# A damped-attention tower on one core: the two terms of the weighted sum in column halves, the sine product on GpSimd, all rows normalised on VectorE

## The reference, cut to what matters

```python
def qrt_damping(x):
    return jnp.sin(C1 * x) * jnp.exp(-(x * x) / PHI) + jnp.cos(C2 * x)
def ttt_filter(scores):
    int_scores = (jnp.abs(scores) * PHI_INT).astype(jnp.int32)
    mod9 = int_scores % 9
    chaos = (mod9 == 0) | (mod9 == 3) | (mod9 == 6)
    return scores * jnp.where(chaos, PHI_INV, 1.0)
...
scores = ttt_filter(jnp.einsum('bhqd,bhkd->bhqk', q, k) / 8)
attn = jax.nn.softmax(scores, axis=-1)
attn = attn * qrt_damping(attn)
ctx = jnp.einsum('bhqk,bhkd->bhqd', attn, v)
```

## Time and profile before

| | |
|---|---|
| median of 3 runs | 6793.55 us (6787.77 to 19916.96) |
| the profiled execution | 6774.6 us |
| its span in the profile | 6772.9 us |
| granted TensorE clock, mean | 0.892 of full speed |
| DMA, whole span | 48.46 MB, 7 GB/s |

### The profile page before, as it was taken

One profiled execution on the slowest core, in us unless ns is written; L12 is line 12 of the kernel. 1 busy time (PEld: TensorE's weight loads), 2 busy tenths in 40 slices (PEclk: granted clock), 3 DMA queues, 4 the chain that ended last, 5 costly groups with the idle time before them and its releaser, 6 DMA issues. The chain is left out here.

```text
span 6772.9 us, 115321 instructions
## 1 busy us (share of the span) xinstructions
PE 5442.1 (80%) x32426; PEld 3955.2 (58%) x32489; DVE 5082.3 (75%) x10177; ACT 4262.2 (63%) x7370; POOL 2754.5 (41%) x2639
## 2 busy tenths in 40 slices
PE   2788877787777877877888777778787799997999
PEld 1455555555555555555655555555555577775777
DVE  1888888888888888888888888888888555555443
ACT  1677777777777777777777777777777322222222
POOL 4445554444555544444555444445554200100111
PEclk9888898989889888888888889888988799898999
DMA  1000000000000000000000000000000000000000
GB/s 17 12 8 7 7 7 7 7 7 10 7 7 7 7 7 7 7 9 9 7 7 7 7 7 7 9 9 7 7 7 4 8 1 2 1 1 13 4 6 6
DMA packets 34500, 48.46 MB, mean 7 GB/s; under 512 B 24473, under 2 KB 24537, under 8 KB 34010
## 3 DMA queue, kind: packets, MB, share of 16 engines
q1 hardware_dynamic: 31962, 43.49, 2.5%
q0 software_dynamic: 2048, 0.14, 0.1%
HBM read 39.40 MB, written 4.19 MB: 6 GB/s over the span
## 5 line engine op out<-in xcount | busy, mean ns | idle before, releaser
L571 PE MATMUL banks<-ident,att 128*128 128x128 f32 x8192 | 1458.9, 311 | 873.6 <-DVE ag L508 496.8
L571 PEld LDWEIGHTS banks<-ident,att 128*128 128x128 f32 x8192 | 1024.2, 159 | 1568.6 <-DVE ag L508 1044.0
L377 POOL TENSOR_TENSOR sinb<-sinb,work 128x512 f32<-128x512 f32 x1024 | 1289.3, 1272 | 900.3 <-DVE sinb L482 898.3
L599 PE MATMUL banks<-kT,qT 128*128 128x512 f32 x2048 | 1262.5, 702 | 113.9 <-ACT att L423 104.0
L387 POOL TENSOR_SCALAR wgt<-wgt 128x512 f32<-128x512 f32 x1024 | 700.2, 684 | 1586.7 <-DVE wgt L502 1581.4
L635 PEld LDWEIGHTS outp<-vo,sinb 128*128 128x128 f32 x8192 | 1164.7, 216 | 214.9 <-issue 185.3
L635 PE MATMUL outp<-vo,sinb 128*128 128x64 f32 x8192 | 1162.6, 295 | 1.9 <-ACT att L423 1.9
L476 DVE TENSOR_TENSOR work<-banks,work 128x512 f32<-128x512 f32 x1024 | 699.8, 689 | 254.0 <-ACT work L435 183.6
L451 ACT ACTIVATE work<-banks 128x512 f32<-128x512 f32 x1024 | 609.9, 596 | 420.4 <-PE banks L571 411.6
L458 ACT ACTIVATE mag<-banks 128x512 f32<-128x512 f32 x1024 | 606.4, 594 | 356.2 <-PE banks L599 350.0
L435 ACT ACTIVATE work<-banks,halfpi 128x512 f32<-128x512 f32 x1024 | 695.4, 685 | 208.9 <-PE banks L571 139.6
(11 more groups left out here) (194 smaller groups left out, 6740.6 us busy)
## 6 DMA issues: line engine op xcount, KB each, us to landing
xq<-xT_dram SPq DMA_DIRECT2D x64, 256.0 KB
xv<-xT_dram SPq DMA_DIRECT2D x64, 256.0 KB, 3.7
xT_dram<-xT SPq DMA_DIRECT2D x8, 256.0 KB, 2.9
out<-hres SPq DMA_DIRECT2D x8, 256.0 KB, 2.6
base<-in_L_tok_turns,idx POOLq DMA_INDIRECT x64
wqk<-in_L_attn_Wq SPq DMA_DIRECT2D x64, 16.0 KB
wqk<-in_L_attn_Wk SPq DMA_DIRECT2D x64, 16.0 KB
wqk<-in_L_attn_bq SPq DMA_DIRECT2D x64, 0.2 KB
```

Source lines behind the costliest of these rows:

```text
L377: nc.gpsimd.tensor_tensor(sinb[:, k % RING], sinb[:, k % RING], work[:, k % RING], ALU.add).then_inc(summed, 1)
L571: mm = nc.tensor.matmul(bank[:, i * P:(i + 1) * P], att[:, p, 4 * half + i, kt * P:(kt + 1) * P], ident[:], is_transpose=True, start=(i == ...
L599: nc.tensor.matmul(score_bank(n), qT[:, p, (n // 2) * P:(n // 2 + 1) * P], kT[:, p, (n % 2) * 512:(n % 2 + 1) * 512], start=True, stop=Tru ...
```

## The change

1. The weighted sum. The value block `vo[:, kt]` becomes the stationary operand (64 columns), and `work` (cosine term) and `sinb` (sine term) are each streamed whole, 512 columns; the first goes to rows 0 to 63 of `outp`, the second to rows 64 to 127. GpSimd's sum of the terms is gone. A tile k now has key block k % 8 and query half k // 8, so `outp` holds one query half at a time and is taken out twice a head (OUT): copied to `acc` for an even head, added to it for an odd head. Every second head `acc` is multiplied with `pair` (two identities on top of each other), which adds the two terms and transposes back (FOLD, 8 matmuls), and VectorE adds the result to `hres` (ADD).
2. The sine goes to `sinb` in SBUF; the bank is free once the sine has read it. GpSimd multiplies `sinb` by `ag`, VectorE's L482 is gone.
3. VectorE normalises all eight rows; the rounding of turns starts one step earlier (TURNS). GpSimd's L382 is gone.
4. The schedule: projections at steps 24 and 26 instead of 18 and 20, values at 29 instead of 25, AV at steps 34 to 41 and then 44, 46 to 58.
5. `kT` has one buffer for both parities, the other head's rows meeting zeros of `qT`.

The diff, cut to its core:

```diff
+        kT = sb("kT", [P, S])
+        acc = sb("acc", [P, 2, 512])
+        pair = sb("pair", [P, D])
...
-        PROJ, VAL = 18, 25 + STEPS
+        PROJ, VAL = 24, 29 + STEPS
...
-        AV = [SINE + 6 + 8 * k // 5 for k in range(NTILE)]
-        OUT = AV[-1] + 1
+        AV = [SINE + 6 + k if k < TB else SINE + 16 + 2 * (k - TB) for k in range(NTILE)]
+        OUT = (AV[TB - 1] + 1, AV[-1] + 1)
+        FOLD, ADD = OUT[1] + 1, OUT[1] + 2
...
-        TURNS = EXP + 3
-        DVE_ROWS = (TB // 2 - 1, TB - 1)
+        TURNS = EXP + 2
...
+        def folds(g, p):
+
+            if isinstance(g, int):
+                return g // 2
+            return (g - p) // 2
...
-                        k = a - SINE - 5
+                        k = a - SINE - 4
                         if 0 <= k < NTILE:
-
-                            wait(pool, tmul, NTILE * g + k + 1)
-                            nc.gpsimd.tensor_tensor(sinb[:, k % RING], sinb[:, k % RING], work[:, k % RING],
-                                                    ALU.add).then_inc(summed, 1)
-                        j = a - EXP - 1
-                        if 0 <= j < TB and j not in DVE_ROWS:
-                            held(pool, recip, TB * g + j + 1)
-                            nc.gpsimd.tensor_scalar(att[:, p, j], att[:, p, j], rs[:, j:j + 1], TURN,
-                                                    ALU.mult, ALU.mult).then_inc(weights, 1)
+                            wait(pool, sined, NTILE * g + k + 1)
+                            wait(pool, agd, NTILE * (g + 1))
+                            nc.gpsimd.tensor_tensor(sinb[:, k % RING], sinb[:, k % RING], ag[:, k],
+                                                    ALU.mult).then_inc(tmul, 1)
...
                 if c == 0:
-                    wait(act, qk, NTILE * (g - 1))
+                    wait(act, qk, NTILE * g)
                 cols = slice(c * 512, (c + 1) * 512)
-                nc.scalar.activation(qT[0:D, p, cols], outp[0:D], ACT.Copy, scale=QSCALE).then_inc(qk_sb, 1)
-                nc.scalar.activation(kT[0:D, p, cols], outp[D:P], ACT.Copy).then_inc(qk_sb, 1)
+                rows = slice(p * D, (p + 1) * D)
+                nc.scalar.activation(qT[rows, p, cols], outp[0:D], ACT.Copy, scale=QSCALE).then_inc(qk_sb, 1)
+                nc.scalar.activation(kT[rows, cols], outp[D:P], ACT.Copy).then_inc(qk_sb, 1)
...
                             wait(act, nned, NTILE * g + k + 1)
-                            nc.scalar.activation(sine_bank(k), sine_bank(k), ACT.Sin,
+                            wait(act, av, NTILE * g + k - RING + 1)
+                            nc.scalar.activation(sinb[:, k % RING], sine_bank(k), ACT.Sin,
                                                  scale=2.0 * math.pi * (1.0 - 2.0 ** -22)).then_inc(sined, 1)
...
-                        k = a - SINE - 4
-                        if 0 <= k < NTILE:
-                            wait(dve, sined, NTILE * g + k + 1)
-                            wait(dve, av, NTILE * g + k - RING + 1)
-                            nc.vector.tensor_tensor(sinb[:, k % RING], sine_bank(k), ag[:, k],
-                                                    ALU.mult).then_inc(tmul, 1)
-                        if a == OUT:
-                            wait(dve, av, NTILE * (g + 1))
+                        if a in OUT:
+                            half = OUT.index(a)
+                            wait(dve, av, NTILE * g + TB * (half + 1))
+                            if p == 0:
+                                nc.vector.tensor_copy(acc[:, half], outp[:]).then_inc(evac, 1)
+                            else:
+                                nc.vector.tensor_tensor(acc[:, half], outp[:], acc[:, half], ALU.add).then_inc(evac, 1)
+                        if a == ADD and p == 1:
+                            wait(dve, folded, folds(g, p) + 1)
...
                         j = a - EXP - 1
-                        if j in DVE_ROWS:
+                        if 0 <= j < TB:
...
-                            wait(pe, turned, TB * (g + 1))
-                            kt, half = k // 2, k % 2
+                            wait(pe, turned, TB * g + 4 * (k // TB) + 4)
+                            kt, half = k % TB, k // TB
...
                             else:
-                                wait(pe, tmul, NTILE * g + k - 3)
-                            fill(g, p, sine_bank(k), k // 2, k % 2)
+                                wait(pe, sined, NTILE * g + k - 3)
+                            fill(g, p, sine_bank(k), k % TB, k // TB)
                         if a in AV:
                             k = AV.index(a)
-
-                            wait(pe, summed, NTILE * g + k + 1)
+                            kt, half = k % TB, k // TB
+
+                            wait(pe, acd, NTILE * g + k + 1)
+                            wait(pe, tmul, NTILE * g + k + 1)
                             if k == 0:
                                 wait(pe, v_sb, g + 1)
-                            kt, half = k // 2, k % 2
-                            for i in range(4):
-                                o = (4 * half + i) * D
-                                mm = nc.tensor.matmul(outp[:, o:o + D], sinb[:, k % RING, i * P:(i + 1) * P],
-                                                      vo[:, kt, :], start=(k == 0 and i == 0),
-                                                      stop=(k >= NTILE - 2), skip_group_check=True)
+                            if k == TB:
+                                wait(pe, evac, 2 * g + 1)
+                            for term, rows in ((work, slice(0, D)), (sinb, slice(D, P))):
+                                mm = nc.tensor.matmul(outp[rows], vo[:, kt, :], term[:, k % RING],
+                                                      start=(kt == 0), stop=(kt == TB - 1), skip_group_check=True)
                             mm.then_inc(av, 1)
+                        if a == FOLD and p == 1:
+                            wait(pe, evac, 2 * g + 2)
+                            for j in range(TB):
+                                mm = nc.tensor.matmul(outp[:, j * D:(j + 1) * D],
+                                                      acc[:, j // 4, j % 4 * P:(j % 4 + 1) * P], pair[:],
+                                                      start=True, stop=True)
+                            mm.then_inc(folded, 1)
```

54 lines of the change are left out of this document (27 added, 27 removed).

## The result

The changed kernel takes 7005.77 us (median of 4 executions, 6994.67 to 7016.7) where the kernel before took 6790.66 beside it: a ratio of 1.032, 95% interval 1.0298 to 1.0342, slower. The profiled execution took 7007.41 us with a span of 7005.7, at a mean granted clock of 0.907 (0.892 before). The forecast was 7037, and 3.6% slower.

The account below looks back on a forecast made before the run. No single bound: VectorE in its full stretch, no engine in the sine stretch, then ScalarE. Terms −0.9 + 1.9 + 1.8 + 0.6 + 0.4 = +3.8 us a head, × 64 = 243, gave 7037 us; range 6700 to 7310.

Parts of the forecast that it names:

- TensorE becomes the bound of the steps with sums: Sine stretch, eight steps with a weighted sum: TensorE needs 2.05 us a step, more than ScalarE's 1.22; +1.8 us a head.
- The sum at 1.29 us, the step at 2.05: Sine stretch: only the middle two of four passes overlap, 1.29 us; with subtraction, fill and gaps 2.05 us a step.
- Rival 2: Weighted sum: both column halves pair fully, 0.9 us a sum; +0.4 us a head, 6820 us, no difference; chance 0.14.
- The value projection at +1.9: Start of the sines: values between fills 1 and 2 put the third cosine 4.75 us after the table load, against 2.84.
- The tail at −0.9: End of the gauss work: values leave, projection copies come in; sine table load at 3047.5 instead of 3048.41, −0.9 us a head.
- 0.35 of waiting for fill 14: Gauss tail: ScalarE's wait for that fill before the sine table load, counted as 0.35 us.
- The fold at +0.4: Eight TensorE matmuls every second head, ahead of a fill and a score: 0.9 us each time, +0.4 us a head.
- VectorE's stretch at +0.6: VectorE's full stretch: six more rows +4.0, hidden −1.9, evacuations +0.3, contention returned 1.8; +0.6 us a head, between −0.6 and +2.4.
- Rival 1: Weighted sum: column halves do not overlap, 1.72 us a sum, step 2.48; 7.65 us a head, 7284 us; chance 0.23.
- Rival 3: Sine stretch: TensorE drains at each switch of width, 0.16 us, two a step; 6.4 us a head, 7203 us; chance 0.05.
- Rival 4: Sine stretch: TensorE never becomes the bound, ScalarE's 1.22 us a step rules; −3.3 us a head, 6600 us; chance 0.15.

Follow-up runs that it names:

- the control: The kernel before with only the value projection cut in four pieces at steps 17 to 20, query/key projections at 22 and 24: 6721.68 us, ratio 0.9897.

## Why the prediction was right

It was right in sign, and in the mechanism that it is named for: TensorE is the bound of the steps with sums, and the values cost time in their new place. That the size is right within half a per cent is luck: three of its terms were wrong by 1.3, 1.5 and 2.4 us a head, and the errors cancelled.

- **TensorE becomes the bound of the steps with sums: right.** One half for both terms costs 0.86 a step in full, GpSimd's product elsewhere costs nothing, thinner sums bring the step down.
- **The sum at 1.29 us, the step at 2.05: mis-sized.** The sentence that failed is "with halves that run side by side only the middle two meet". Two f32 matmuls in different halves issue first, first, second, second, 0.01 us apart, so all passes meet in pairs: 2 × 0.43 and the changes of width, and a step of 1.79. From the third cosine to the exponential table load, a head lost 0.61 instead of gaining 1.8. That is the largest error of the three, 2.4. Rival 2 had this mechanism, and its "Against it" (passes issued two by two for one half) is what the trace refutes. Its time of 6820 did not come because of the next two points. The rule of the Trainium skill ("TensorE: Matmul & The Clock Gate", "Part 3: Packing small matmuls") that matmuls in different column groups run concurrently agrees with the 0.01 us; the forecast applied it matmul by matmul, while the records go pass by pass.
- **The value projection at +1.9: right in mechanism, mis-sized.** It measured +3.16. The forecast took its prices from one head of the kernel before: third cosine at 2.84 before, and after at 1.25 to the start of the values, 2.85 for them and 0.65 for the fill, 4.75. Over 55 heads the place before is 2.65, and after it is 5.80: 1.49, 3.13 and 1.18. Block and fill both run near half clock there. The prices were read at one place and carried to another, colder one.
- **The tail at −0.9: wrong.** It came out +0.60. The values left it, but the projections that took their place ran in part at half clock (1.91 us at 3084.50) with ScalarE's copies in line behind them. Two steps failed, by about 0.75 each. One is "0.35 of waiting for fill 14": from the exponential that the forecast counts from to the table load it is 6.96 in the mean of 55 heads instead of 6.2, of which ScalarE waits 0.98; in the shown head it waits 0.47 for a fill and 0.45 for the projection, which its copy needs. The other is the head that was taken as the kernel before: there that stretch was 3048.41 − 3041.30 = 7.11, over 55 heads it is 6.36, where the values took 2.85 to the next fill in that head and 2.18 in the mean. There was less to win than one head showed; on the kernel before, taking the values out and splitting them won 0.57 of the tail.
- **The fold at +0.4: right.** In the changed kernel round 4 to 8 takes 0.77 more in every second head, the one with a fold.
- **VectorE's stretch at +0.6: near.** From the exponential table load to the last filter the pieces sum to +0.40, the fold's 0.4 among them, so the six rows and what is given back cancel: 0.0, inside the bounds of −0.6 and +2.4. That nothing is not the price of the rows: alone on the kernel before they cost VectorE 0.46, and given back on the last kernels 0.43. What in the change takes the difference back is not shown.
- **Rival 1 (no overlap)** is what the run with one half shows, 7474 where the rival said 7284, 3.0 us a head more: eight steps priced at 2.48 against 2.63 are 1.2 of it, the values at 1.9 against 3.16 are 1.3. **Rival 3 (a drain at each switch)** came at most in part: a step of 1.79, less 0.86 for the pass pairs, 0.22 for the subtraction and 0.49 for the fill, leaves 0.22 for both switches and every gap, where the forecast had 0.05 and the rival two drains of 0.16 besides. The pairs at 0.43 without a change of width and at 0.48 and 0.54 beside one place about 0.2 of it at the two changes, 0.1 each. The rule of the Trainium skill ("TensorEngine Tiling (Array Packing)", "Key Properties") that a change of mode drains TensorE fits that remainder; these runs do not tell a drain from another price of the change. **Rival 4 (TensorE never bound)** failed as argued: 512 columns did not pass in under 0.43. (Its sum counts the 19 us twice: 6774.6 − 211 + 19 is 6582, not 6600.) Its gain on the chain was real, though, and shows once the sums are thinned and the values hidden: 2.1% under the kernel before (6633 us; the interval, 0.976 to 0.9815, leaves open whether it is 2%), and 2.7% with six rows given back (6600). Of the 2.4 us a head of the first figure, about 0.7 is the place of the values, which the kernel before can have without the rest of the change (the control).

Sum by the forecast's steps, measured: tail +0.60, third cosine +3.16, from there to the exponential load −0.61, VectorE +0.40 with the fold in it: +3.55, and 3.53 head to head.

## What to carry to other kernels

When a block of matmuls is moved, price it at the granted clock of the place it goes to, over many heads and not one, and look for a loop whose bound is another engine, where it can be laid in pieces no longer than TensorE's wait in that loop. Relief given to a chain shows only where no other engine is full in the same steps, so count what the step asks of TensorE after the edit, and spread it before judging the edit. Two 64-column f32 streams in column halves cost no more than one, but the change to half width and back cost about 0.2 us here, which sums laid next to each other would pay once (a whole kernel ordered so was not run).

## What the runs showed of the hardware that was not expected

- Two f32 matmuls of 512 columns in the two column halves interleave by pass and take 1.02 us to the next instruction, against 1.86 in one half (3002.75 to 3004.61); one alone takes 1.00 (the run with one term). In a row of sums a pair of passes costs 0.43; a change to half width and back costs about 0.2 besides.
- VectorE and GpSimd slow each other when both read two SBUF tiles: 0.67 to 1.16 us and 1.27 to 1.72. The Trainium skill, "SBUF — State Buffer", "SBUF: two separate sides", calls the port they share an exclusive lock, with the other engine blocked for the whole instruction. The rows agree with it nearly: both get slower, the instruction with a PSUM operand escapes, and the two fall into one pace. But that pace is 1.68, where one strictly after the other would be 0.67 + 1.27 = 1.94 by their durations alone, so they overlap by a part.
- The granted clock depends on the order of the work: the same 16 passes ran at half clock in 28% of the records in the gauss tail, 87% after it, and in none when they lay in pieces between scores in the kernel before.
